# A cross-attention layer on one core: how keys reach the matmul layout and how the attention result is written

## What is computed

```python
x = x + xattn(layernorm(x), ctx_1024, mask)     # 16 heads of 16 channels, 64 queries on 1601 keys
x = x + span_attention(layernorm(x))            # attention by learned position spans
x = x + ffn(layernorm(x))                       # a shared MLP and 8 experts

# xattn:
qh, kh, vh = split_heads(q @ wq.T + bq), split_heads(k @ wk.T + bk), split_heads(v @ wv.T + bv)
scores = einsum('bhqd,bhkd->bhqk', qh, kh) / sqrt(16)
attn = softmax(where(mask, scores, -1e9))
out = einsum('bhqk,bhkd->bhqd', attn, vh)       # heads joined to 256 channels
return out @ wo.T + bo
```

## Time and profile before

| | before |
|---|---|
| median of 3 runs | 1698.44 us |
| the profiled execution | 1696.06 us |
| its span, first to last instruction | 1694.2 us |
| PE (matmul) busy | 1546.1 us, 91% |
| DVE (VectorE) busy | 1047.3 us, 62% |
| ACT (ScalarE) busy | 916.2 us, 54% |
| POOL (GpSimd) busy | 425.4 us, 25% |
| mean granted PE clock | 0.974 of 2.4 GHz |
| DMA, mean over the span | 93 GB/s |

### The profile page before, as it was taken

One profiled execution on the slowest core, in us unless ns is written; L12 is line 12 of the kernel. 1 busy time (PEld: TensorE's weight loads), 2 busy tenths in 40 slices (PEclk: granted clock), 3 DMA queues, 4 the chain that ended last, 5 costly groups with the idle time before them and its releaser, 6 DMA issues. The chain is left out here.

```text
span 1694.2 us, 56731 instructions
## 1 busy us (share of the span) xinstructions
PE 1546.1 (91%) x23644; PEld 1261.0 (74%) x23644; DVE 1047.3 (62%) x3925; ACT 916.2 (54%) x1832; POOL 425.4 (25%) x549
## 2 busy tenths in 40 slices
PE   7699999999999999999999999999999857877997
PEld 2578888888888888888888888888888723333997
DVE  5666666666666666666666666666666536653543
ACT  4355555555555555555555555555555624554653
POOL 0033233222222222332332323322222030000520
PEclk9799999999999999999999999999999977988999
DMA  5433333444444444444443333344443241000111
GB/s 144 137 102 102 103 103 103 113 126 114 108 111 108 113 111 111 109 112 104 104 104 103 103 103 103 103 111 123 116 111 72 51 124 26 1 1 1 51 32 50
DMA packets 101904, 157.94 MB, mean 93 GB/s; under 512 B 56943, under 2 KB 65903, under 8 KB 101376
## 3 DMA queue, kind: packets, MB, share of 16 engines
q1 hardware_dynamic: 101456, 153.69, 34.3%
q0 software_dynamic: 192, 0.59, 0.1%
HBM read 69.17 MB, written 4.19 MB: 43 GB/s over the span
## 5 line engine op out<-in xcount | busy, mean ns | idle before, releaser
L674 DVE CUSTOM_DVE_ANT_0 junk<-bank,mask_q 128x400 bf16<-128x400 f32 (+1 forms) x1024 | 558.7, 571 | 116.2 <-issue 109.8
L626 ACT ACTIVATE probs<-bank 128x512 f32<-128x512 f32 (+1 forms) x832 | 450.7, 595 | 273.1 <-PE bank L786 257.8
L665 DVE SCALAR_TENSOR_TENSOR k_lo<-bank,bk,k_hi 128x400 f16<-128x400 f32 (+1 forms) x256 | 162.5, 635 | 313.2 <-ACT k_hi L636 313.2
L767 PE MATMUL bank<-kstack,qstack 96*128 96x400 f16 (+1 forms) x1024 | 308.0, 339 | 49.9 <-DVE part_max L674 42.1
L602 POOL CAST ctx_hi<-ctx_raw 128x400 fp32r<-128x400 f32 x248 | 121.5, 519 | 919.7 <-PE bank L750 919.7
L750 PE MATMUL bank<-wv_hi,ctx_hi 128*128 128x256 f32 (+1 forms) x832 | 283.4, 341 | 0.0
L786 PE MATMUL bank<-qstack,kstack 104*128 104x128 f16 (+1 forms) x3328 | 258.0, 220 | 4.2 <-ACT probs L626 3.6
L605 POOL TENSOR_TENSOR ctx_lo<-ctx_raw,ctx_hi 128x400 fp32r<-128x400 f32 x248 | 253.2, 1041 | 0.0
L786 PEld LDWEIGHTS bank<-qstack,kstack 104*128 104x128 f16 (+1 forms) x3328 | 206.0, 99 | 56.0 <-issue 28.1
L636 ACT ACTIVATE k_hi<-bank,bk 128x400 f16<-128x400 f32 (+1 forms) x256 | 152.1, 594 | 172.0 <-PE bank L740 169.2
L750 PE MATMUL bank<-wv_lo,ctx_hi 128*128 128x256 f32 (+1 forms) x832 | 233.5, 281 | 0.0
(11 more groups left out here) (165 smaller groups left out, 1753.9 us busy)
## 6 DMA issues: line engine op xcount, KB each, us to landing
ctx_raw<-in_ctxT SPq DMA_DIRECT2D x32, 1602.0 KB, 6.9
kstack<-k_hi SPq DMA_DIRECT2D x512, 100.1 KB, 2.2
kstack<-k_lo SPq DMA_DIRECT2D x256, 100.1 KB, 2.5
weight<-in_w SPq DMA_DIRECT2D x18, 256.0 KB, 2.7
x<-in_xT SPq DMA_DIRECT2D x8, 512.0 KB, 6.3
attn_out<-o_norm SPq DMA_DIRECT2D x256, 8.0 KB, 1.8
qstack<-q_parts SPq DMA_DIRECT2D x192, 16.0 KB
out_yT<-x SPq DMA_DIRECT2D x1, 2048.0 KB, 6.4
```

What stands on the lines that cost most here:

```text
L626: nc.scalar.activation(probs[kt % NP][0:m, GROUPS * h:GROUPS * (h + 1), :], st[h][0:m, :], ACT.Exp, scale=DK ** -0.5 / (UP * UP)).then_inc ...
L665: nc.vector.scalar_tensor_tensor(k_lo[:, t, s0:s0 + n], pj[(b.slot + c) % 2][:, 0:n], w["bk"][:, t:t + 1], k_hi[:, t, s0:s0 + n], ALU.add, ...
L674: nc.vector.tensor_tensor_reduce(junk[(b.slot + i) % 2][:, 0:n], sm[(b.slot + i) % 2][:, 0:n], w["mask_q"][:, s0:s0 + n], 1.0, -3.0e38, AL ...
L767: nc.tensor.matmul(sm[(b.slot + i) % 2][:, 0:n], qstack[b.slot][0:KSTACK, p, :], kstack[b.slot][0:KSTACK, p, s0:s0 + n], start=True, stop= ...
```

## The change

Two things are changed. **Keys:** the channels of the key projection are permuted on the host, so that partition 4r + g of a half holds channel r of pair g. One transfer then takes all 128 partitions of a half to 32 partitions with 4 rows each; three transfers a half, one semaphore a half. M 0 waits for all of half 0, M 16 for all of half 1. **Result:** `outputs` picks the result and the sums of both heads by a mask of rows, and writes `attn_out` itself; `o_norm`, the stores and their semaphores are gone, and the tail waits for `out_done`. One small constant is loaded at the start.

```diff
@@ queries, sync
             load(bo[:], ins["bo"], wo_in)
+            load(w["half_rows"][:], ins["c_half_rows"], wo_in)
@@ cross_attention, sync
             sp.wait_ge(klo_done, NCK * b.n + KC * (t + 1))
-            for g in range(GROUPS):
-                p = GROUPS * t + g
-                for i, part in enumerate((k_hi, k_lo, k_hi)):
-                    sp.dma_start(kstack[b.slot][32 * i:32 * i + 32, p, :],
-                                 part[32 * g:32 * g + 32, t, :]).then_inc(kstack_in[b.slot][p], 16)
-
-        def store(b):
-
-            sp.wait_ge(out_done, b.n + 1)
-            for g in range(GROUPS):
-                for e in range(2):
-                    rows = slice(32 * g + DK * e, 32 * g + DK * (e + 1))
-                    sp.dma_start(attn_out[rows, :, bass.ds(b.n * S, S)], o_norm[b.slot][rows, e::2, :]).then_inc(attn_st[b.slot], 16)
-
+            for i, part in enumerate((k_hi, k_lo, k_hi)):
+                sp.dma_start(kstack[b.slot][32 * i:32 * i + 32, GROUPS * t:GROUPS * (t + 1), :],
+                             part[:, t, :]).then_inc(kstack_in[b.slot][t], 16)
...
-            if cur and cur.n >= 2:
-                store(at(cur.n - 2))
...
-        for n in (B - 2, B - 1):
-            store(at(n))
@@ cross_attention, scalar
-                for p in range(GROUPS * t, GROUPS * (t + 1)):
-                    need(act, kstack_in[1 - b.slot][p], 16 * STACK_DMAS * (b.used - 1 + b.slot))
+                need(act, kstack_in[1 - b.slot][t], 16 * STACK_DMAS * (b.used - 1 + b.slot))
@@ cross_attention, vector
         def outputs(b):
-            o = ob[b.slot][:, 0:GROUPS * S].rearrange("p (t c) -> p t c", t=GROUPS)
+            o = [ob[b.slot][:, 0:GROUPS * S].rearrange("p (k e c) -> p k e c", k=NK, e=2)[:, :, e, :] for e in range(2)]
+            low, high = w["half_rows"][:, 0:1], w["half_rows"][:, 1:2]
             dve.wait_ge(pv_done, KT * (b.n + 1))
-            for e in range(2):
-                nc.vector.stream_shuffle(sums[:, e::2, :], o[:, e::2, :], [DK * (1 - e) + i % DK for i in range(32)]).then_inc(sums_done, 1)
-            dve.wait_ge(sums_done, 2 * (b.n + 1))
-            nc.vector.reciprocal(rsum[:], sums[:]).then_inc(rsum_done, 1)
+            nc.vector.tensor_scalar(o_half[:], o[1], high, None, ALU.mult).then_inc(halves_done, 1)
+            nc.vector.tensor_scalar(sum_half[:], o[0], high, None, ALU.mult).then_inc(halves_done, 1)
+            dve.wait_ge(halves_done, 2 * (b.n + 1))
+            nc.vector.scalar_tensor_tensor(o_both[:], o[0], low, o_half[:], ALU.mult, ALU.add).then_inc(both_done, 1)
+            nc.vector.scalar_tensor_tensor(sum_both[:], o[1], low, sum_half[:], ALU.mult, ALU.add).then_inc(both_done, 1)
+            dve.wait_ge(both_done, 2 * (b.n + 1))
+            nc.vector.stream_shuffle(sum_half[:], sum_both[:], [(i + DK) % 32 for i in range(32)]).then_inc(sums_done, 1)
+            dve.wait_ge(sums_done, b.n + 1)
+            nc.vector.reciprocal(rsum[:], sum_half[:]).then_inc(rsum_done, 1)
             dve.wait_ge(rsum_done, b.n + 1)
-
-            need(dve, attn_st[b.slot], 16 * STORE_DMAS * (b.used - 1))
-            nc.vector.tensor_tensor(o_norm[b.slot][:], o, rsum[:], ALU.mult).then_inc(out_done, 1)
+            nc.vector.tensor_tensor(attn_out[:, :, b.n * S:(b.n + 1) * S], o_both[:], rsum[:], ALU.mult).then_inc(out_done, 1)
@@ cross_attention, tensor (chunk_scores)
-            if i % KC == 0:
-                pe.wait_ge(kstack_in[b.slot][p], 16 * STACK_DMAS * b.used)
+            if i % (NMX // NK) == 0:
+                pe.wait_ge(kstack_in[b.slot][p // GROUPS], 16 * STACK_DMAS * b.used)
@@ tail (output_a)
-            for stored in attn_st:
-                pe.wait_ge(stored, 16 * STORE_DMAS * (CB // 2) * (c + 1))
+            pe.wait_ge(out_done, CB * (c + 1))
@@ host
+    stacked = np.arange(D).reshape(NK, GROUPS, P // GROUPS).transpose(0, 2, 1).reshape(-1)
...
+        "c_half_rows": (rows[:, None] % 32 // DK == np.arange(2)[None]).astype(np.float32),
...
-        "wkT": a["L0_xattn_wk_w"].T,  "bk": cols(a["L0_xattn_wk_b"]),
+        "wkT": a["L0_xattn_wk_w"][stacked].T,  "bk": cols(a["L0_xattn_wk_b"][stacked]),
```

More of the change, by code:

```diff
@@ L120, in build @@
         bo_all = ctx.enter_context(nc.sbuf_tensor("bo_all", [P, NK], F32))
-        attn_st = [sem(f"attn_st{i}") for i in range(2)]
+        out_done = sem("out_done")
         eps_col = ctx.enter_context(nc.sbuf_tensor("eps_col", [P, 1], F32))
@@ L130, in build @@
                 bk=sb("bk", [P, NK], F32), bv=sb("bv", [P, NK], F32),
+                half_rows=sb("half_rows", [P, 2], F32),
                 mask_q=sb("mask_q", [P, S2], BF16), mask_k=sb("mask_k", [P, KT, S], BF16),
@@ L146, in build @@
             before, ready = queries(nc, ins, bank, w, first_in, wo, bo, bo_all, wo_in, ident, mean_w, eps_col, q_parts, sem)
-            cross = cross_attention(nc, sb, ins, bank, w, first_in, attn_out, attn_st, q_parts, sem)
+            cross = cross_attention(nc, sb, ins, bank, w, first_in, attn_out, out_done, q_parts, sem)
             def both(eng, name):
@@ L176, in _ @@
                     both(pe, "tensor")
-        tail(nc, ins, bank, attn_out, attn_st, wo, bo_all, mean_w, eps_col, out_dram, sem)
+        tail(nc, ins, bank, attn_out, out_done, wo, bo_all, mean_w, eps_col, out_dram, sem)
 def run_periods(order, table):
@@ L442, in tensor @@
             run_periods(PE_ORDER, {"M": (0, means, None), "V": (1, variances, None), "P": (2, project, None)})
-            pe.wait_ge(wo_in, 2 * 16)
+            pe.wait_ge(wo_in, 3 * 16)
             pe.wait_ge(w_in, 4 * 16)
@@ L453, in queries, with cross_attention @@
         return {"sync": sync, "vector": vector, "gpsimd": gpsimd, "scalar": scalar, "tensor": tensor}, ready
-def cross_attention(nc, sb, ins, bank, w, first_in, attn_out, attn_st, q_parts, sem):
+def cross_attention(nc, sb, ins, bank, w, first_in, attn_out, out_done, q_parts, sem):
     raw, c_hi, c_lo, kstack, qstack = (first_in[n] for n in ("raw", "c_hi", "c_lo", "kstack", "qstack"))
@@ L470, in cross_attention @@
     row_max = sb("row_max", [P, PAIRS], F32)
-    sums = sb("sums", [P, GROUPS, S], F32)
-    rsum = sb("rsum", [P, GROUPS, S], F32)
-    o_norm = [sb(f"o_norm{i}", [P, GROUPS, S], F32) for i in range(2)]
+    o_half = sb("o_half", [P, NK, S], F32)
+    o_both = sb("o_both", [P, NK, S], F32)
+    sum_half = sb("sum_half", [P, NK, S], F32)
+    sum_both = sb("sum_both", [P, NK, S], F32)
+    rsum = sb("rsum", [P, NK, S], F32)
     pj = bank[0:2]
@@ L485, in cross_attention @@
     v_ones = sem("v_ones")
-    kstack_in = [[sem(f"kstack_in{i}{p}") for p in range(PAIRS)] for i in range(2)]
+    kstack_in = [[sem(f"kstack_in{i}{t}") for t in range(NK)] for i in range(2)]
     qstack_in = [sem(f"qstack_in{i}") for i in range(2)]
@@ L495, in cross_attention @@
     pv_done = sem("pv_done")
+    halves_done = sem("halves_done")
+    both_done = sem("both_done")
     sums_done = sem("sums_done")
     rsum_done = sem("rsum_done")
-    out_done = sem("out_done")
     STACK_DMAS = 3
@@ L840, in cross_attention, with tail @@
     return {"sync": sync, "vector": vector, "gpsimd": gpsimd, "scalar": scalar, "tensor": tensor}
-def tail(nc, ins, bank, attn_out, attn_st, wo, bo_all, mean_w, eps_col, out_dram, sem):
+def tail(nc, ins, bank, attn_out, out_done, wo, bo_all, mean_w, eps_col, out_dram, sem):
     with ExitStack() as own:
@@ L871, in tail @@
             with ExitStack() as span:
-                spans = span_attention(nc, span, bank, sem, mean_w, eps_col, attn_out, attn_st, x, h2, wo, bo_all, wspan, wval, wout,
+                spans = span_attention(nc, span, bank, sem, mean_w, eps_col, attn_out, out_done, x, h2, wo, bo_all, wspan, wval, wout,
                                        sel_a, sel_b, head_ones, x_in, w_in, sel_in, h2_done)
@@ L936, in _, with span_attention @@
                 mlps["tensor"](pe)
-def span_attention(nc, own, bank, sem, mean_w, eps_col, attn_out, attn_st, x, h2, wo, bo_all, wspan, wval, wout,
+def span_attention(nc, own, bank, sem, mean_w, eps_col, attn_out, out_done, x, h2, wo, bo_all, wspan, wval, wout,
                    sel_a, sel_b, head_ones, x_in, w_in, sel_in, h2_done):
@@ L1540 @@
         "maskT": maskT,
-        "wqT": a["L0_xattn_wq_w"].T, "wkT": a["L0_xattn_wk_w"].T, "wvT": a["L0_xattn_wv_w"].T, "woT": a["L0_xattn_wo_w"].T,
-        "bq": cols(a["L0_xattn_wq_b"]), "bk": cols(a["L0_xattn_wk_b"]), "bv": cols(a["L0_xattn_wv_b"]), "bo": cols(a["L0_xattn_wo_b"]),
+        "wqT": a["L0_xattn_wq_w"].T, "wkT": a["L0_xattn_wk_w"][stacked].T, "wvT": a["L0_xattn_wv_w"].T, "woT": a["L0_xattn_wo_w"].T,
+        "bq": cols(a["L0_xattn_wq_b"]), "bk": cols(a["L0_xattn_wk_b"][stacked]), "bv": cols(a["L0_xattn_wv_b"]), "bo": cols(a["L0_xattn_wo_b"]),
         "wspanT": np.concatenate([span[0::2], np.zeros((SOFT_ROW - H, D), np.float32), span[1::2]]).T,
```

1 line of the change is left out of this document (removed).

## The result

The changed kernel takes **2002.47 us** (median of 4 runs, 1995.59 to 2005.20); the kernel before takes 1699.14 us on the same chip (4 runs, 1698.11 to 1707.05). The ratio is 1.177, 95% interval 1.175 to 1.180: slower, as forecast, but by 303 us where 41 were forecast, and far outside the range.

A forecast was written before the change was run, and what follows sets the result against it. PE, busy nine tenths of the span, was taken as the bound. Late keys +27.6 and +2.1, clock +17, stage end -5.7 gave +41 on 1696.06 us: 1737; with the runs' median 2.4 higher, 1739 was said; range 1691 to 1772.

The forecast's parts named there:

- M 0 would wait for the half: Attention turn on PE: M 0 starts at 630.39 in place of 628.50, PE's turn queued behind; +0.89 us a turn.
- the old wait ahead of M 2: Attention turn on PE: today's wait of 1.06 us before M 2 is swallowed by the new wait for keys.
- the chain on DVE: Attention result on DVE: the new operations take perhaps 2.9 us against 2.79 today, at no cost.
- the end of the stage: From the last attention product to the tail: without stores the tail begins at 1364.04, -5.7 us.
- no cost of the removed issues: SyncE's queue: the 18 issues a turn that go cost nothing today, so removing them changes no time.
- the sign: Whole kernel: slower, with a chance of 0.81; same 0.04, faster 0.15.
- I take 232 because its row is the same copy: Key transfers: 1.23 MB of a half move at 232 GB/s in 5.3 us, arriving at 630.39.
- The test against the stores: Key rate: stores in 256-byte pieces reach 186 GB/s when full, so the gap is no fixed cost per small piece.
- Rival C: Key transfers: copy slower than now, 160 GB/s, +3.3 us a turn, clock falls in most turns, above 1800 us; chance 0.05.
- The clock: PE after its 1.9 us wait: clock falls in half of 31 turns at 1.1 us each, +17 us.
- The 218 GB/s for a band: Key transfers: the skill's limit for partitions 0 to 31; the half takes 5.6 us, sum about 11 us higher.
- rival A: Key transfers: large ones run above 279 GB/s, no turn loses anything, 1692.7 us; chance 0.17.

The follow-up runs named there:

- warm_wait: The changed kernel with 45 matmuls of 400 columns, their result unread, ahead of PE's wait for half 0; 1967.03 us.
- result_only: The changed kernel with the keys moved as before (12 transfers a half, channels not permuted); 1695.61 us, ratio 0.9973 to the kernel before.
- the single copies: Three kernels: result_only plus extra copies of data no longer needed ahead of the tail, each waited for; 1740.26, 1747.82 and 1802.71 us.
- spread_two: two_pairs with the three parts of the key and query stacks interleaved, so destinations spread over 96 partitions; 1695.66 us, ratio 0.9969 to the kernel before.
- two_pairs: The changed kernel with six key transfers a half, 64 source partitions to 32, PE waiting for three ahead of M 0 and of M 8; 1804.8 us.
- spread_stack: The changed kernel with the three parts of the key and query stacks interleaved, so destinations spread over 96 partitions; 1823.68 us, ratio 1.072 to the kernel before.
- wait_half: result_only, its 12 small transfers kept, but PE waits for all four pairs of a half ahead of M 0; 1883.87 us.

## Why the prediction was wrong

**Right.** That M 0 would wait for the half and all of PE's turn behind it; that the old wait ahead of M 2 would be swallowed and its 1.1 us with it (2.02 us from M 0 to M 2 became 1.02 in warm_wait, at full clock); the chain on DVE, 2.92 for 2.9 us; the end of the stage, -6.0 us of PE's idle time in result_only for -5.7; no cost of the removed issues; the sign.

**The step that failed: "I take 232 because its row is the same copy".** It was not the same copy. The row showed 32 adjacent partitions into 32, and the change reads 128 partitions into 32. "Since the destination stays 32 partitions" took the destination alone for the limit; the single copies show that both sides count: 204 GB/s matched, 106 from 128. For its own shape the row of 232 was 14 to 20% too high (204 and 193 GB/s). M 0 came 13.7 us after the first issue for the forecast 7.06, thus 8.5 us later than before in place of 1.9, and less the swallowed wait this costs some 7.5 us a turn in place of 0.89. The test against the stores (small pieces are not slow) was sound, and was about another thing. Rival C had the mechanism, 128 source partitions in front of few destinations, with a chance of 0.05, and took 160 GB/s for its bottom; but that rate was set by the issues of SyncE's queue, not by the copy, and so was no bound. With 106 GB/s the working of the forecast gives 1.2 MB / 106 = 11.3 us of data and, with 1.76, 13.1 us from the first issue to M 0; measured 13.7. What is left may be half 1, whose transfers go out from about 667 on and share the engines; that was not tried.

**The clock.** Both parts of the term were too small: 31 x 0.5 x 1.1 = 17 us for some 65. The price of a fall was some 2.1 us, above the 1.7 that the prediction took for the most: the low clock lasted 4.9 us behind M 0 in the mean, where 2.8 had been read from turn -1. The count was all 32 turns and not half. The longer the wait ahead of M 0 (its median), the more of the 32 turns had the low clock at some time within 6 us of M 0:

```
kernel         idle, us    turns with a fall
spread_two       0.25         1
two_pairs        2.39        18
spread_stack     3.26        27
wait_half        4.99        32
after            8.40        32
```

At a wait like the 1.9 us forecast half would have been near the truth: of the six turns of two_pairs with 1.73 to 2.29 us three had a fall. But the prediction had taken it only as the middle between none and all; that is luck more than reading. This term is 48 us of the miss of 262; the late keys are the rest.

**The two figures of the Trainium skill.** The 218 GB/s for a band ("SBUF — State Buffer", "Door 1: The DMA port swizzle") gave a sum 11 us higher and would have been as wrong. The 2.0 us plus bytes at 436 GB/s of rival A ("DMA: Bandwidth & Descriptors", "Anatomy of one DMA", for GpSimd's path) give 2.9 us for one copy of 0.4 MB; from 128 to 128 partitions it took 2.64, from 128 to 0-31 5.38.

## What to carry to other kernels

A DMA inside SBUF is priced by both of its sides: before small transfers are joined into a large one, see whether both of its sides are spread over the partitions alike, and if one side has few partitions, spread those. Count what the consumer waits for, too: small transfers with a semaphore each deliver the first piece early, and joining them (or just their waits) moves the first use behind the last byte. A rate seen in a stretch where issues set the pace is no bound for a copy of another form.

## What was not expected of the hardware

- A copy between spread partitions and a narrow band ran at 105 to 124 GB/s in either direction, about half of the 183 to 204 of a narrow copy into a narrow band, with all 16 DMA engines shown busy in the kernel (share 1.02 at 119 GB/s). A busy share near 1 does not say that the engines move much.
- Rows from 128 partitions into 32 went at 367 GB/s where the 32 were every fourth of 128, and at 106 where they were adjacent.
- The small copy from every fourth partition was slower alone (125 GB/s against 204), yet its packets were shorter (0.129 us against 0.232) and it cost nothing in the kernel. The length of a packet in the trace is not its share of the time to landing.
- Why spread to narrow falls to half the rate of the band, and 0-63 to 0-31 with it, stays open.
